# A macaron network: every expert on every token, or the chosen experts on gathered rows

## The reference

```
x = x + 0.5 * moe(LN(x))            # first expert stage
x = x + attention(LN(x))            # 16 heads of 16, full softmax over 2048 tokens
x = x + 0.5 * moe(LN(x))            # second expert stage
x = x + 0.5 * lstm(LN(x))           # two time steps: the two sequences
x = x + causal_attention(LN(x))     # rotary, relative positions
x = x + 0.5 * lstm(LN(x))

def moe(x):                         # gate_w 6 x 256; each of the 7 experts has three 256 x 256 matrices
    probs = sigmoid(x @ gate_w.T + gate_b)
    w, idx = top_k(probs, 2);  w = w / (sum(w) + 1e-8)
    ge = zeros(T, 6) with w at idx
    y = sum over e of ge[:, e] * ((silu(x @ ew1[e].T) * (x @ ew3[e].T)) @ ew2[e].T)
    return y + (silu(x @ fc1.T) * (x @ fc2.T)) @ fc3.T        # the shared expert
```

## Time and profile before

| | us |
|---|---|
| runs shown, median (lowest to highest) of 3 | 4698.61 (4684.21 to 4701.09) |
| the profiled execution, and its span | 4671.09, 4669.5 |
| first expert stage, from its first statistics | 16.6 to 542.3 |
| QKV of full attention | 543 to 630 |
| heads and projection of full attention | 633 to 2176 |
| second expert stage | 2177.4 to 2699.2 |
| first LSTM stage | 2699.8 to 2918 |
| causal attention, second LSTM stage | 2918 to 4655 |
| output | 4655.4 to 4669.5 |

### The profile page before, as it was taken

How to read it: one execution, slowest core, us unless ns; L and a number is a source line. 1 busy time by engine, 2 the same in 40 slices (tenths; PEclk the granted TensorE clock), 3 DMA queues, 4 the chain that set the end, 5 groups by cost and what they waited for, 6 DMA issues and landing times. The chain is left out here.

```text
span 4669.5 us, 79371 instructions
## 1 busy us (share of the span) xinstructions
PE 4239.2 (91%) x25648; PEld 2522.6 (54%) x25648; DVE 3004.6 (64%) x5513; ACT 2295.4 (49%) x4375; POOL 682.8 (15%) x698
## 2 busy tenths in 40 slices
PE   7999969999999999986999989639999999997688
PEld 6888743333333333324888855525656656654454
DVE  5556668888888888835656533746666666663432
ACT  3222317777777777761332222214656556655222
POOL 2232200000000000000233200532222222220000
PEclk9999979999999999987999999868999989998789
DMA  2000172323323322203000000476667667662401
GB/s 85 0 0 0 52 146 38 46 34 43 46 34 44 46 38 39 32 6 120 8 0 0 1 20 0 150 198 179 188 176 184 188 165 186 191 158 52 131 20 36
DMA packets 173944, 359.15 MB, mean 77 GB/s; under 512 B 40586, under 2 KB 104714, under 8 KB 156810
## 3 DMA queue, kind: packets, MB, share of 16 engines
q1 hardware_dynamic: 154634, 304.20, 28.5%
q0 software_dynamic: 18944, 50.35, 3.9%
HBM read 209.71 MB, written 152.06 MB: 77 GB/s over the span
## 5 line engine op out<-in xcount | busy, mean ns | idle before, releaser
L1314 DVE TENSOR_REDUCE full_tops<-psum 128x1 f32<-128x1024 f32 x1024 | 1206.2, 1218 | 184.0 <-PE psum L1218 184.0
L1271 ACT ACTIVATE full_probs<-psum 128x512 f32<-128x512 f32 x2048 | 1065.8, 602 | 299.2 <-PE psum L1190 295.1
L1781 ACT ACTIVATE causal_probs<-psum 128x512 f32<-128x512 f32 (+3 forms) x1280 | 640.2, 533 | 397.9 <-PE psum L1653 230.0
L1190 PE MATMUL psum<-full_q,full_k 49*128 49x512 f32 x2048 | 653.3, 475 | 23.2 <-ACT full_probs L1271 17.2
L1832 DVE TENSOR_REDUCE causal_tops<-psum 128x1 f32<-128x1024 f32 (+7 forms) x704 | 586.8, 857 | 112.6 <-PE psum L1704 112.6
L1190 PEld LDWEIGHTS psum<-full_q,full_k 49*128 49x128 f32 x2048 | 284.5, 186 | 605.8 <-ACT full_probs L1271 576.9
L1199 PE MATMUL psum<-full_probs,full_vh 128*32 128x512 f32 x4096 | 556.8, 616 | 0.7 <-ACT full_probs L1271 0.7
L1218 PE MATMUL psum<-full_k,full_q 48*128 48x512 f32 x2048 | 402.0, 458 | 51.4 <-DMA full_k<-qk_split 23.6
L1653 PE MATMUL psum<-causal_q,causal_k 49*128 49x512 f32 (+3 forms) x1280 | 407.7, 451 | 14.2 <-ACT causal_probs L1781 8.3
L1704 PE MATMUL psum<-causal_k,causal_q 48*128 48x512 f32 (+4 forms) x1152 | 325.3, 414 | 70.2 <-DVE causal_tops L1847 33.4
L274 POOL TENSOR_TENSOR moe_h_lo<-moe_h,moe_h_hi 128x512 fp32r<-128x512 f32 x224 | 290.3, 1296 | 661.2 <-ACT moe_h_hi L387 661.2
(11 more groups left out here) (190 smaller groups left out, 6070.7 us busy)
## 6 DMA issues: line engine op xcount, KB each, us to landing
causal_bias<-bias_tiles SPq DMA_DIRECT2D x32, 1280.0 KB, 6.3
band_scores<-xn POOLq DMA_DIRECT2D x256, 160.0 KB, 4.2
full_q<-qk_split SPq DMA_DIRECT2D x192, 128.0 KB, 6.3
full_k<-qk_split SPq DMA_DIRECT2D x192, 128.0 KB, 7.1
causal_q<-rot_parts SPq DMA_DIRECT2D x192, 128.0 KB, 5.4
causal_k<-rot_parts SPq DMA_DIRECT2D x192, 128.0 KB, 6.4
bias_tiles<-causal_skew_rows SPq DMA_DIRECT2D x32, 640.5 KB, 3.4
bias_tiles<-causal_skew_rows SPq DMA_DIRECT2D x32, 640.0 KB, 3.3
```

The lines of the kernel that those rows point to most:

```text
L1190: nc.tensor.matmul(k.psum[:, b, :], k_sb[at, q, kt * P:(kt + 1) * P], q_sb[at, q, n * BLK:(n + 1) * BLK], start=True, stop=True).then_inc( ...
L1271: nc.scalar.activation(pT[:, kt % 4, n * BLK:(n + 1) * BLK], k.psum[:, bank(q, u), :], ACT.Exp).then_inc(p_ready, 1)
L1314: nc.vector.reduce_max(mx[:, q % 2, u // 2, u % 2:u % 2 + 1], src, AX_X).then_inc(m_free, 1)
L1781: nc.scalar.activation(dst, k.psum[:, bank(q, u), 0:(hi - lo) * P], ACT.Exp).then_inc(p_ready, 1)
```

## The change

**Expert stages.** A stage now has two parts. In the first, each of the 8 blocks runs the shared expert alone (`rest`, `hidden`, `update`), the gate (now split in high and low parts, L479) and the routing: `choose` finds the two best experts, `weigh` the weights, `positions` (PE) counts how many tokens each expert has had so far, `locate` gives each token a slot in its expert's list, and POOL scatters the token's number to both slots in DRAM (L406: 8 indirect DMAs a block, 128 numbers of 4 bytes each). SP stores the normalised rows to DRAM. `schedule` turns the counts into a table of 21 blocks of 512 slots (`NX` = 16 + 5), each with its expert. In the second part, SP reads the table, loads the block's expert weights (768 KB) and its token numbers; POOL gathers the 512 rows with 4 indirect DMAs (L418); ACT and DVE split the weights again for each block; PE runs `up` and `down`; ACT copies the result (L616), and SP stores it. All 21 blocks run, whatever the data.

**The stage behind adds.** `Returns` brings both expert outputs of a tile back to a ring of 8 tiles (`pool_bring`, L937: 2 indirect DMAs of 128 rows of 1 KB a tile, 64 a stage) and adds them to x with their weights (`dve_add`, L946, L951: 2 instructions of 256 columns a tile), ahead of the statistics: in `qkv_full_stage` and in the first `lstm_stage`.

**Overlaps between stages.** The load of x waits only for the identity; each part of x is awaited where it is read. In `qkv_full_stage`, POOL sets `full_k` and `full_vh`, and SP loads heads 0 to 2 between the stores of blocks 5 to 7. The sums of the first sequence are inverted at the end of the heads; the projection's first two loads no longer stand behind the reciprocals. The last LSTM stage stores x by blocks. The touched loops of the expert stages, of QKV and partly of the LSTM are written out (`straight`, `straight_ahead`).

```diff
+NX = 16 + E - 1
+NV = NBLK + NX
...
-                for e in range(E + 1):
-                    if e >= 2:
-                        sp.wait_ge(w_lo, e - 1)
-                    sp.dma_start(w_in[:, e % 2, :], io["moe_w"][:, e * NW:(e + 1) * NW]).then_inc(s_in[e % 2], 16)
...
+                sp.wait_ge(plan_ready, 1)
+                for b in range(2):
+                    load_weights(b)
+                sp.wait_ge(k.scattered, scattered_all())
+                for b in range(4):
+                    load_ids(b)
+                load_weights(2)
+                for v in range(NBLK, NV + 1):
+                    if v >= NBLK + 1:
+                        store(v - NBLK - 1)
+                    if v - 5 < NX:
+                        load_weights(v - 5)
+                    if v - 4 < NX:
+                        load_ids(v - 4)
...
+                    for t in range(n * TB, (n + 1) * TB):
+                        for s in range(2):
+                            pool.indirect_dma_start(
+                                out=k.TOKENS[:, :], out_offset=bass.IndirectOffsetOnAxis(ap=idx[:, s, t:t + 1], axis=0),
+                                in_=token[:, t:t + 1], in_offset=None).then_inc(k.scattered, 16)
...
+                    for t in range(TB):
+                        pool.indirect_dma_start(
+                            out=xg[:, b % 4, t, :], out_offset=None, in_=k.XN[:, :],
+                            in_offset=bass.IndirectOffsetOnAxis(ap=idr[:, b % 6, t:t + 1], axis=0)).then_inc(k.gathered[b % 4], 16)
...
+                for v in range(NBLK - 2):
+                    up(v + 1, 0, (0,))
+                    positions(v + 1)
+                    up(v + 1, 0, (1,))
+                    transpose(v + 2)
+                    up(v + 1, 1)
+                    gate(v + 2)
+                    down(v, 0)
+                    gate_transpose(v + 2)
+                    down(v, 1)
...
+                for v in range(NBLK, NV):
+                    if v + 1 < NV:
+                        up(v + 1, 0)
+                    if v + 2 < NV:
+                        transpose(v + 2)
+                    if v + 1 < NV:
+                        up(v + 1, 1)
+                    down(v, 0)
+                    down(v, 1)
...
+                for v in range(NBLK - 2):
+                    locate(v + 1)
+                    hidden(v + 1, 0)
+                    lower_x(v + 2)
+                    if v + 3 < NBLK:
+                        apply(v + 3)
+                    hidden(v + 1, 1)
+                    choose(v + 2)
+                    weigh(v + 2)
+                    update(v)
+                    if v + 4 < NBLK:
+                        stats(v + 4)
...
+    def pool_bring(self, pool, first, count):
+        k = self.k
+        for i in range(first, first + count):
+            if i >= 8:
+                pool.wait_ge(k.added, self.run * TT + i - 7)
...
+                for n in range(half, NBLK):
+                    for u in range(NU):
+                        store(n, u)
+                    load_full_head(k, sp, F, n - half, n - half)
...
+                ret.pool_bring(pool, 0, 2 * TB)
                 ln.pool_rstd(pool, 0, 0)
+                ret.pool_bring(pool, 2 * TB, TB)
                 ln.pool_rstd(pool, 1, 1)
+                ret.pool_bring(pool, 3 * TB, TB)
...
-            with sp.Fori(0, NBLK // 2) as it:
+            load(0, 0)
+            load(1, 1)
+            sp.wait_ge(s_rc, 1)
...
             def normalize(n):
+                if ret:
+                    ret.dve_add(dve, n * 2 * TB, 2 * TB)
+                    dve.wait_ge(k.added, ret.run * TT + (n + 1) * 2 * TB)
...
+STAGES = [moe_then(0, ROW_ORDER, full_attention), moe_then(1, PAIR_ORDER, lstm(0)), causal_attention, lstm(1)]
```

947 lines of the change are left out of this document (660 added, 287 removed).

## The result

The changed kernel takes 4540.55 us (median of 4 runs, 4529.53 to 4549.64), the one before 4694.46 (4 runs, 4684.21 to 4701.09): a ratio of 0.9682, 95% interval [0.9655, 0.9709], 154 us faster. The forecast was 4457, range 4370 to 4590. The time lies in the range, but 242 us were forecast. The profiled executions have spans of 4669.5 and 4536.8: 133 us, so 109 of the forecast gain are missing, and this part is about where.

The account below looks back on a forecast made before the run. Expert stages were taken as bound by PE's matmul count. Terms -134 - 130 + 35 - 8 - 9 + 14 - 10 = -242 took 4671.1 to 4429; the median's 27.5 more gave 4457 us, range 4370 to 4590.

Parts of the forecast that it names:

- rival (2): POOL bounds some stages at 1.6 to 2.2 us an indirect DMA; at 2.0, +130 us, 4587; chance 0.18.
- 27 of 56 units gone: Expert stages: 29 units of PE work for 56, by PE alone 225 us less a stage, 450 in all.
- The price of an indirect DMA: POOL's scatters and gathers: taken as 1.14 us each, lower bound 0.73, upper 2.0.
- Rivals (1): POOL's descriptors decide everywhere: 3 us an indirect DMA, +506 us, 4963; chance 0.10 together with other slower waits.
- Shared round 16.7: Shared blocks of an expert stage: a circle of DVE, PE and ACT takes 16.7 us a round, PE needing 12.7.
- rival (4): Granted clock may fall in shared rounds: 20 us a round instead of 16.7, +46 us, 4503; chance 0.08.
- Routed block 10.4: Routed blocks: ACT and DVE in one circle take 10.4 us a block, PE needing 9.4; 20 blocks 208 us.
- rival (3): ACT and DVE circle doesn't bind; routed blocks run at PE's 9.4 us: -40 us, 4417; chance 0.15.
- The gap: Between shared and routed blocks: scatters, three landings at about 2.5 us each, gathers, transposes: 25 us without PE work.
- QKV +35: QKV of full attention: returned adds make DVE the bound at 11 us a block, later start; 122 us against 87.
- Heads -8: Head loads between QKV's stores: last stores 13 us later, PE's 23.62 us wait shrinks to about 2; net -8 us.
- LSTM, adds hidden in DVE's wait: First LSTM: 16 adds a block (7 us) fit DVE's 10.30 us wait, costing nothing; up to 28 without that gap.

Follow-up runs that it names:

- runs 5 and 11: 5: changed kernel with shared-block scatters around both h_lo, 4573.29 us; 11: also last scatters, routed gathers, QKV memsets and head loads moved, 4504.60 us.
- run 4: Changed kernel with h_lo of the routed blocks made on DVE instead of POOL: 4536.30 us.
- run 6: Changed kernel with the loads for the first heads behind all QKV stores instead of between them: 4573.40 us.

## Why the prediction was right, and what it missed

The time lies in the range, but not by the mechanism that the range's upper part stood for: 4590 came from rival (2), dear indirect DMAs, and these were cheap. Only 154 of the 242 us came.

- *27 of 56 units gone*: right. PE's busy time fell by 181 and 177 us in the two expert stages.
- *The price of an indirect DMA*: taken 1.14 us, measured 0.96 busy and 1.26 from one to the next. Rivals (1) and (2) fall with it, except where POOL has nothing but such DMAs: in QKV 11.4 us a block by POOL instead of 11 by DVE.
- *Shared round 16.7*: the unlocked round is 16.4 to 16.5 (runs 5 and 11), so the circle was sized rightly. The step that failed is that it "fills" DVE's list with durations of operations standing alone. From the second choosing to the eighth 113.8 us pass in each stage, where six rounds were forecast at 95. Of the 38 us missing in both stages 24 are the eight comparisons held by POOL (3.0 each). The others are the first of the six, 20.9 and 21.2 us with no comparison held, whose cause stays open, and last rounds that get less short than forecast.
- *The clock*, rival (4), did not lengthen the rounds: the four of 19.5 and 17.9 us in the first stage had granted clocks of 0.91, 1.00, 0.83 and 0.90, and the one at 1.00 took 19.5 like the one at 0.83.
- *Routed block 10.4, bound by the circle of ACT and DVE*: wrong in what binds. Without the lock PE binds at 9.90, which is rival (3) with 0.5 more than its 9.4; with it DVE's wait gives 11.14. That the two errors nearly cancel is luck: the 21 blocks took 237 us and 230, where 230 were forecast. The circle itself showed at 10.51, in run 4.
- *The gap*: scatters and gathers were right (1.26 each), the three landings were not. 7.5 us were taken from the least landing of the earlier trace rows; the waits are 15.0 + 6.7 in the first stage and 12.1 + 6.6 in the second: 25 us missing in all. A landing that takes 2.3 at the least in the trace of before is not what a chain pays that goes through the scatters' writes, SP's load and 128-row gathers; the median there, 4.7, would have given 14 in each stage, and 21.7 and 18.7 were needed.
- *QKV +35*: measured +41 to PE's last product. The memsets were counted as time of POOL; that they hold DVE as well was not.
- *Heads -8*: the wrong sign. PE's wait ahead of them was to shrink from 23.6 us by 8 and grew to 26.6, since the loads stand between the stores; in run 6 it is 17.4. The heads themselves took 6.5 us longer, nearly all of it in their last part (granted clock 0.95 for 0.97 there); the cause stays open.
- *Projection -9*: -9.0. *Out -10*: -11.6. *LSTM, adds hidden in DVE's wait*: right, 211.3 us against 211.0, though DVE has 19 us more. The way into it was 29.8 us from the last product of the experts (copied at 2548.5) to the first statistics at 2578.3, some 5 more than forecast: 4.5 until POOL's first gather, 19.7 for the 16 gathers, 5.5 for the landing and the last adds.
- *The rest*: in the first stage 3 us more than in the second from the last choosing to h_lo (13.6 and 10.6), where DVE and ACT stand still. Causal attention took 8.3 more with the same code and work; it takes 1532 to 1553 us in the thirteen profiles of the changed kernel and its variants, and 1525 in the one of before. Its granted clock was 0.91 before and 0.90 or 0.89 after. Whether that is chance between executions the single profile of before can't say. With 38 us in the rounds, 25 for the landings, 7 for the routed blocks, 6 in QKV, 17 in the heads, 5 on the way into the LSTM, 3 and 8 here, the 109 us have a place; what is behind some 30 of them stays open, as said.

The lock could have been read from the trace of before. There the weights are split once a stage, and three of seven L484 a stage are longer than 1.76, each beside an h_lo; and the maximum of 2469 ns for L126 in the earlier trace rows is one that begins 0.16 us behind weights lo at 44.30:

```profile
44.46 2.47 POOL L126 TENSOR_TENSOR lnv<-lnv,neghalf 128x4 f32<-128x4 f32 x1 [0.79 <-DVE lnv L120]
...
50.72 1.30 POOL L274 TENSOR_TENSOR moe_h_lo<-moe_h,moe_h_hi 128x512 fp32r<-128x512 f32 x1 [1.31 <-ACT moe_h_hi L387]
51.47 2.17 DVE L484 TENSOR_TENSOR moe_w_lo<-moe_w_in,moe_w_hi 128x1536 fp32r<-128x1536 f32 x1
```
